# Layer 0's experts in a four-layer network: every expert's second product, or only the two that each image chose, fetched by register

## The reference

```
logits = jnp.mean(x, axis=1) @ Wr + br
routing_weights = jax.nn.softmax(logits, axis=-1)
scale = jnp.where(expected_loads > capacity, capacity / expected_loads, 1.0)
routing_weights = jax.nn.softmax(routing_weights * scale, axis=-1)
rw_tok = jnp.broadcast_to(routing_weights[:, None, :], (B, S, E)).reshape(N, E)
top_w, top_i = jax.lax.top_k(rw_tok, K)
top_w = jax.nn.softmax(top_w, axis=-1)
xf = x.reshape(N, D)
h = jax.nn.gelu(jnp.einsum('nd,edf->enf', xf, W1) + b1[:, None, :], approximate=False)
y = jnp.einsum('enf,efd->end', h, W2) + b2[:, None, :]
w_dense = jnp.zeros((N, E), x.dtype).at[jnp.arange(N)[:, None], top_i].add(top_w)
out = jnp.einsum('ne,end->nd', w_dense, y).reshape(B, S, D)
out = _layer_norm(out + x, gamma, beta)
```

## Time and profile before

| what | value |
|---|---|
| median of three runs | 211.53 us (211.3 to 212.07) |
| the profiled execution | 211.5 us, its span 209.7 us |
| TensorE busy | 195.9 us, 93% of the span |
| VectorE, ScalarE, GpSimd busy | 124.5, 129.3, 42.5 us |
| granted TensorE clock | 1.00 on average |
| logits of layer 0 to the first matmul of its norm 2 | 20.38 to 40.84 us |

### The profile page before, as it was taken

How to read it: one execution, slowest core, us unless ns; L and a number is a source line. 1 busy time by engine, 2 the same in 40 slices (tenths; PEclk the granted TensorE clock), 3 DMA queues, 4 the chain that set the end, 5 groups by cost and what they waited for, 6 DMA issues and landing times.

```text
span 209.7 us, 3083 instructions
## 1 busy us (share of the span) xinstructions
PE 195.9 (93%) x1112; PEld 91.5 (44%) x1120; DVE 124.5 (59%) x364; ACT 129.3 (62%) x216; POOL 42.5 (20%) x60
## 2 busy tenths in 40 slices
PE   7998999999999998999999999999998997799993
PEld 2654222348876764322222363532234594333221
DVE  0466879957641824945342547595455688586435
ACT  2535688646355683776575830688685675598682
POOL 7761000000000000103963000100920011010740
PEclk9999999999999999999999999999999999999999
DMA  6999300000000000000000000000000000000001
GB/s 228 355 407 404 123 0 2 0 0 3 2 3 0 3 0 0 0 5 0 0 0 0 0 3 0 0 0 0 0 6 0 2 0 3 0 0 0 3 0 50
DMA packets 3119, 8.40 MB, mean 40 GB/s; under 512 B 550, under 2 KB 1072, under 8 KB 2976
## 3 DMA queue, kind: packets, MB, share of 16 engines
q1 hardware_dynamic: 2736, 7.60, 9.7%
q0 software_dynamic: 224, 0.46, 0.6%
q10 hardware_dynamic: 144, 0.13, 0.2%
HBM read 7.94 MB, written 0.26 MB: 39 GB/s over the span
## 4 chain that ended last, share of the span: by engine, by line
PE 78%; DVE 10%; ACT 8%; issue 3%; DVEq 0%; ACTq 0%
PE bank L362 17%; PE banks L379 9%; PE banks L291 8%; PE banks L380 7%; PE banks L555 6%; PE bank L302 5%; PE bank L296 4%; ACT hidden L727 3%; PE bank L343 3%; PE banks L516 2%; PE banks L497 2%; PE bank L612 2%; PE bank L480 2%; PE bank L325 2%; ACT rstd L689 1%
## 5 line engine op out<-in xcount | busy, mean ns | idle before, releaser
L727 ACT ACTIVATE hidden<-banks,pack_l 128x1024 f32<-128x1024 f32 (+1 forms) x43 | 44.9, 1052 | 18.3 <-PE banks L380 17.8
L362 PE MATMUL bank<-hidden,w 128*64 128x512 f32 (+1 forms) x160 | 41.4, 596 | 1.3 <-ACT hidden L727 1.3
L291 PE MATMUL banks<-idle_work 128*128 128x512 bf16 x116 | 31.1, 401 | 2.0 <-DVE idle_work L1000 1.2
L379 PE MATMUL banks<-split_x,w_hi 128*128 128x512 f16 x80 | 30.7, 384 | 0.0
L380 PE MATMUL banks<-split_x,w_lo 128*128 128x512 f16 x80 | 30.3, 379 | 0.0
L1442 POOL CAST split_x<-normed 64x256 f16<-64x256 f32 x8 | 4.0, 494 | 99.7 <-DVE normed L896 95.2
L685 ACT ACTIVATE squares<-bank 128x256 f32<-128x256 f32 x18 | 6.9, 383 | 22.5 <-PE bank L296 22.4
L379 PEld LDWEIGHTS banks<-split_x,w_hi 128*128 128x128 f16 x80 | 7.7, 97 | 28.4 <-issue 11.5
L291 PEld LDWEIGHTS banks<-idle_work 128*128 128x128 bf16 x123 | 12.4, 105 | 16.2 <-issue 5.0
L1451 POOL TENSOR_TENSOR total<-total,term 128x512 f32<-128x512 f32 x12 | 17.6, 1463 | 2.6 <-DVE term L982 2.0
L362 PEld LDWEIGHTS bank<-hidden,w 128*64 128x64 f32 x160 | 7.9, 134 | 18.3 <-issue 13.6
(11 more groups left out here) (314 smaller groups left out, 322.3 us busy)
## 6 DMA issues: line engine op xcount, KB each, us to landing
w_stage<-in_w SPq DMA_DIRECT2D x3, 512.0 KB, 13.2
w_stage<-in_w SPq DMA_DIRECT2D x1, 1024.0 KB, 9.6
conv<-in_conv SPq DMA_DIRECT2D x1, 800.0 KB, 7.7
w<-in_w SPq DMA_DIRECT2D x3, 256.0 KB, 13.4
w<-in_w SPq DMA_DIRECT2D x1, 512.0 KB, 10.4
toeplitz<-in_toeplitz SPq DMA_DIRECT2D x1, 512.0 KB, 11.2
gauss<-in_gauss SPq DMA_DIRECT2D x1, 512.0 KB, 12.4
pack_l<-in_pack_l SPq DMA_DIRECT2D x1, 373.5 KB, 14.9
```

The source lines that it names most:

```text
L291: mm(out, idle_work[:, 0:128], idle_work[:, 0:cols], start=True, stop=True)
L362: last = mm(out[64 * h:64 * h + 64, cut], w2[l][:, (f * NE + e) * CH:(f * NE + e + 1) * CH], hidden[v % 3][:, h * 512 + cut.start:h * 512 ...
L379: mm(out, w1_hi[l][:, at:at + 128], split_x[h][:, :], start=True, stop=False)
L727: last = act(hidden[u % 3][:, cut], both[u % 2][:, cut], ACT.Gelu, bias=P(f"l{l}", "e_b1")[:, e * fc + f:e * fc + f + 1])
```

## The change

TensorE's stream for layer 0's experts is a new function, `image_experts`. The first products of all 8 experts are still made; units 0 and 1 use the fp32 weights and `normed[1]` directly (`STRAIGHT = 2`), so that they don't wait for the half-precision parts, and unit 0 stands ahead of the logits matmul. All eight hidden activations are kept, in `l0_hidden`. VectorE finds the two best experts of each image with its sorting and index instructions. GpSimd reads the eight chosen numbers (4 images by 2) into registers and copies for each the 128x64 block of `w2` into a zeroed 128x128 stationary (`w2_pick`); the zero columns let both halves accumulate into one 128-row result. TensorE reads the same eight numbers into registers of its own, and makes eight 256-column fp32 matmuls in place of sixteen 512-column ones; their moving operand's address comes from the register. VectorE weighs four results in place of sixteen. ScalarE has no biases to add and no `split`, which goes wholly to GpSimd; the second bias is brought into norm 2 by two matmuls of its own (L376). One softmax is left out of the routing and replaced by the order of the scaled values and a sigmoid of the gap.

```diff
-        hidden = [sb(f"hidden{i}", [128, 2 * COLS]) for i in range(3)]
+        l0_hidden = sb("l0_hidden", [128, EXPERTS * 2 * COLS])
+        hidden = [l0_hidden[:, i * 2 * COLS:(i + 1) * 2 * COLS] for i in range(3)]
...
+            def image_experts():
+
+                def up(u):
+                    pe.wait_ge(S["w1_loaded0"], 16)
+                    if u == 0:
+                        pe.wait_ge(S["ln_out"], 4)
+                    if u >= 2:
+                        pe.wait_ge(S["moe_gelu"], u - 1)
+                    if u == STRAIGHT:
+                        pe.wait_ge(S["w1_split0"], 2)
+                        pe.wait_ge(S["split_lo"], 4)
+                        for h in range(HALVES):
+                            pe.wait_ge(S[f"split_hi{h}"], 2)
+                    for h in range(HALVES):
+                        r, out = slice(64 * h, 64 * h + 64), both[u % 2][:, h * 512:(h + 1) * 512]
+                        cut = slice(u * 128, u * 128 + 128)
+                        if u < STRAIGHT:
+                            last = mm(out, stage[0][r, cut], normed[1][r, :], start=True, stop=True)
+                        else:
+                            mm(out, w1_hi[0][:, cut], split_x[h][:, :], start=True, stop=False)
+                            last = mm(out, w1_lo[0][:, cut], split_x[h][:, :], start=False, stop=True)
+                    last.then_inc(S["moe_hidden"], 1)
+
+                up(0)
+                pe.wait_ge(S["ones_set"], 1)
+                pe.wait_ge(S["routed"], 2)
+                mm(bank[7][:, 0:INNER * 16], ones[:, :], routed[:, :], start=True, stop=True)\
+                    .then_inc(S["route_logits0"], 1)
+                for u in range(1, NE):
+                    up(u)
+                    busy(1, bank[4][:, :])
+                pe.wait_ge(S["l0_index"], 2)
+                at = {(j, h, n): pe.value_load(own_at[64 * h:64 * h + 1, j * 8 + n:j * 8 + n + 1], min_val=0,
+                                               max_val=NE - 1)
+                      for j in range(INNER) for h in range(HALVES) for n in range(TOP_K)}
+                busy(5, bank[4][:, :])
+                pe.wait_ge(S["moe_gelu"], NE)
+                pe.wait_ge(S["w2_picked"], BATCH * TOP_K)
+                for j in range(INNER):
+                    for n in range(TOP_K):
+                        for h in range(HALVES):
+                            i = (j * HALVES + h) * TOP_K + n
+                            last = mm(picked_y[j][:, n * PIX:(n + 1) * PIX], tile(w2_pick, i),
+                                      l0_hidden[:, bass.ds(at[j, h, n] * (2 * COLS) + (h * COLS + j * PIX), PIX)],
+                                      start=h == 0, stop=h == 1)
+                    last.then_inc(S["l0_down"], 1)
+
+            def norm_of_images():
+
+                pe.wait_ge(S["l0_bias"], 1)
+                for j in range(INNER):
+                    mm(bank[4 + j][:, 0:PIX], P("first", "center"), gap["bias"][:, j:j + 1].broadcast_to([128, PIX]),
+                       start=True, stop=False)
+                for j in range(INNER):
+                    pe.wait_ge(S["l0_term"], 2 * j + 2)
+                    mm(bank[4 + j][:, 0:PIX], P("first", "center"), chunk(total, j), start=False, stop=True)\
+                        .then_inc(S["ln_centered"], 1)
+                averages(2)
...
-            split(1, 0)
...
+            nc.scalar.preload_act_table_set("gelu_and_others")
...
+            image_routing(0)
+            for u in range(NE):
+                sc.wait_ge(S["moe_hidden"], u + 1)
+                act(l0_hidden[:, u * 2 * COLS:(u + 1) * 2 * COLS], both[u % 2][:, :], ACT.Gelu,
+                    bias=P("l0", "e_b1")[:, u:u + 1]).then_inc(S["moe_gelu"], 1)
+                if u in (2, 5):
+                    image_routing((2, 5).index(u) + 1)
...
+            for j in range(INNER):
+                st.mark(V.max(own["sorted"][:, j * 8:j * 8 + 8], own["scaled"][:, j * 8:j * 8 + 8]))
+            ve.wait_ge(st.sem, st.n)
+            TT(g8(own["shifted"][:, :]), g8(own["sorted"][:, :]), g8(own["sorted"][:, :])[:, :, 0:1]
+               .broadcast_to([128, INNER, 8]), ALU.subtract).then_inc(S["l0_exp_in"], 1)
+            for j in range(INNER):
+                V.max_index(own_at[:, j * 8:j * 8 + 8], own["sorted"][:, j * 8:j * 8 + 8], own["scaled"][:, j * 8:j * 8 + 8])\
+                    .then_inc(S["l0_index"], 1)
...
+            for j in range(INNER):
+                ve.wait_ge(S["l0_down"], j + 1)
+                for n in range(TOP_K):
+                    if n:
+                        ve.wait_ge(S["l0_term"], 2 * j + 1)
+                    STT(chunk(total, j), picked_y[j][:, n * PIX:(n + 1) * PIX], pair["weight"][:, j * TOP_K + n:j * TOP_K + n + 1],
+                        chunk(total if n else normed[1], j), ALU.mult, ALU.add).then_inc(S["l0_term"], 1)
...
+            G.memset(w2_pick[:, :], 0.0).then_inc(S["picks_zero"], 1)
...
-            split(1, 0)
+            for j in range(INNER):
+                po.wait_ge(S["ln_out"], 2 * 1 + j + 1)
+                for h in range(HALVES):
+                    r = slice(64 * h, 64 * h + 64)
+                    G.tensor_copy(chunk(split_x[h], j)[r, :], chunk(normed[1], j)[r, :]).then_inc(S[f"split_hi{h}"], 1)
+            po.wait_ge(S["w2_loaded0"], 16)
+            po.wait_ge(S["l0_index"], 2)
+            for j in range(INNER):
+                for h in range(HALVES):
+                    for n in range(TOP_K):
+                        i = (j * HALVES + h) * TOP_K + n
+                        at = po.value_load(own_at[64 * h:64 * h + 1, j * 8 + n:j * 8 + n + 1], min_val=0, max_val=NE - 1)
+                        G.tensor_copy(w2_pick[:, i * 128 + 64 * h:i * 128 + 64 * h + 64], w2[0][:, bass.ds(at * CH, CH)])\
+                            .then_inc(S["w2_picked"], 1)
```

More of the change, by code:

```diff
@@ L167, in metaformer @@
         routed = sb("routed", [128, INNER * 16])
[L168 to L173, removed]
+        l0 = {n: sb(f"l0_{n}", [128, 32]) for n in "logit shifted prob".split()}
+        l0_small = {n: sb(f"l0s_{n}", [128, 8]) for n in "peak sum inv load scale".split()}
+        own = {n: sb(f"own_{n}", [128, INNER * 8]) for n in "scaled sorted shifted exp less inverse index".split()}
+        own_at = sb("own_at", [128, INNER * 8], mybir.dt.uint32)
+        pair = {n: sb(f"pair_{n}", [128, INNER * TOP_K]) for n in "bias weight part".split()}
+        chosen = {n: sb(f"chosen_{n}", [128, INNER * TOP_K * 8]) for n in "mask bias".split()}
+        gap = {n: sb(f"gap_{n}", [128, INNER]) for n in "sum inv less diff tanh bias".split()}
+        relu_sim, sq_sim = (l0_hidden[:, i * 2 * COLS:(i + 2) * 2 * COLS] for i in (3, 5))
         x1_beta = sb("x1_beta", [PART, COLS])
@@ L318, in experts @@
             def experts(l, k):
                 fc, base = fc_of[l], unit_base[l]
[L321 to L328, removed]
+                pe.wait_ge(S["ln_out"], 2 * k + 2)
@@ L329, in experts @@
+                pe.wait_ge(S[f"l{l}_loaded"], 16)
+                for i in range(TILES):
+                    last = mm(bank[7][:, i * 16:(i + 1) * 16], tile(normed[k], i), P(f"l{l}", "router"),
+                              start=True, stop=True)
+                last.then_inc(S["route_logits"], 1)
+                busy(1, bank[0][:, :])
                 pe.wait_ge(S[f"w1_split{l}"], 2)
@@ L427, in _ @@
             norm(1, x[1], x_ready(1))
[L428 to L432, removed]
+            image_experts()
+            norm_of_images()
             for j in range(INNER):
@@ new lines, in _ @@
+            st.mark(rsum(gap["sum"][:, :], g8(ex)))
+            st.link(TS(gap["less"][:, :], ex[:, 1::8], -1.0, 1.0, ALU.mult, ALU.add))
+            st.link(V.reciprocal(gap["inv"][:, :], gap["sum"][:, :]))
+            TT(gap["diff"][:, :], gap["less"][:, :], gap["inv"][:, :], ALU.mult).then_inc(S["l0_exp_in"], 1)
+            ve.wait_ge(S["l0_index"], 2)
+            st.link(V.tensor_copy(own["index"][:, :], own_at[:, :]))
+            masks = lambda n: chosen[n][:, :].rearrange("p (b k e) -> p b k e", b=INNER, k=TOP_K)
@@ new lines, in _ @@
+            st.link(TT(masks("mask"), P("l0", "order").unsqueeze(1).unsqueeze(1).broadcast_to([128, INNER, TOP_K, 8]),
+                       g8(own["index"][:, :])[:, :, 0:TOP_K].unsqueeze(3).broadcast_to([128, INNER, TOP_K, 8]), ALU.is_equal))
+            st.link(TT(g8(chosen["bias"][:, :]), g8(chosen["mask"][:, :]), repeat(P("l0", "e_b2"), INNER * TOP_K), ALU.mult))
+            st.link(rsum(pair["bias"][:, :], g8(chosen["bias"][:, :])))
+            ve.wait_ge(S["l0_exp"], 3)
+            for n in range(TOP_K):
+                st.mark(TS(pair["weight"][:, n::TOP_K], gap["tanh"][:, :], 0.5 - n, 0.5, ALU.mult, ALU.add))
```

111 lines of the change are left out of this document (38 added, 73 removed).

## The result

The changed kernel takes 216.04 us (median of four, 215.4 to 216.2) against 211.42 for the kernel before in its four runs: ratio 1.021, 95% interval 1.019 to 1.024. It is slower by 4.6 us, where 2.2 less was forecast. The profiled execution took 215.4 us, its span 213.6 us, 3.9 more than before.

What follows compares the result with a forecast made beforehand. TensorE was taken as the bound, about 1.95 us per expert. Second products from 34.3 plus 5.4 us put the end of centring at 39.7 against 41.86, so 211.5 - 2.2 = 209.3 us, range 207.4 to 212.9.

Steps and rivals of the forecast that it cites:

- What bounds before, and what the new structure saves: Layer 0's experts: TensorE bounds at about 1.95 us per expert; centring ends 2.2 us earlier and everything behind moves along.
- Up to the indices: Layer 0's routing ahead of the reads: VectorE's first routing instruction at 21.35, `l0_index` complete at 27.3 us.
- The new stall of ScalarE ahead of its second exponential: Behind GELU 2, ScalarE waits for the exponential's input until 26.9: 1.3 us, with TensorE's further units queued behind.
- I assume that its sequencer goes on while the array works through unit 7: TensorE's reads start at 30.4, without waiting for unit 7's matmuls; otherwise 0.8 us more.
- T = 0.35: Time in us of one register read with its two bounds checks; eight in series on TensorE take 2.8 us.
- 5.0 - 8T: Gain in us for T, one checked read's time: used up at T = 0.62, loss over 0.5% from 0.75.
- the dear reads' slower side: Checked reads of 0.75 us or more between unit 7 and the second products: loss over 0.5%, chance 0.07 of 0.18.
- signs of being wrong: New profile: GpSimd's last copy after 34, second products at 32.4, reads of 0.6 or more, clock under 1.00, late `conv_lo`.
- The clock, given 0.08 as a rival by itself: TensorE idle 2.1 us behind unit 7 drops to 1.2 GHz; second products cost 3.45 us more: 212.8 us, chance 0.08.
- From D to C: From the second products' start to the end of layer 0's centring: 5.4 us, VectorE's later jobs just hidden before norm 2.
- GpSimd late: GpSimd's register-addressed copies cost 0.8 in place of 0.25 us, delaying second products to 36.5: 211.5 us, no change, chance 0.07.

Runs made afterwards that it cites:

- e1: The changed kernel with fixed operand addresses in place of TensorE's register reads, so wrong experts are mixed; GpSimd's reads stay: 209.85 us, ratio 0.992 to the kernel before.
- e7: The changed kernel, reads unchecked, TensorE's two behind each of units 4 to 7, logits matmul before unit 0, second exponential behind GELU 3: 206.98 us, ratio 0.977 to before.
- e2: The changed kernel with both bounds checks left out of every register read on TensorE and GpSimd: 211.36 us, ratio 0.999 to the kernel before.
- e9: The changed kernel with 3 and 4 more idle matmuls ahead of TensorE's two waits for VectorE's weights in layer 3: 215.17 us.
- e8: The changed kernel with TensorE reading only the four first choices, checked, each used twice, so second choices are wrong: 210.92 us, ratio 0.996 to the kernel before.

## Why the prediction was wrong, step by step

**What bounds before, and what the new structure saves: right.** TensorE set the pace and the stage's end moved the rest. With no reads on TensorE the time fell below that of before (e1), and with cheap, covered reads to 206.98 against 211.73 (e7).

**Up to the indices: right within 0.3 us.** Logits on VectorE at 21.65 (forecast 21.35), indices complete at 27.41 (27.3). The new stall of ScalarE ahead of its second exponential was 0.76 us, not 1.3, because GELU 2 itself came 0.7 late. GELU 5 ended at 30.69 (30.2), the last at 33.02 (32.4): 0.5 and 0.6 late.

**"I assume that its sequencer goes on while the array works through unit 7": right.** The first read starts with unit 7's first matmul, at 30.86; the forecast had 30.4, and GELU 5's half microsecond is all of the difference.

**"T = 0.35": the step that failed.** A read with its checks measured 0.75 us on TensorE in the changed kernel, and 0.81 on GpSimd. The read alone is 0.465, more than the whole of T, and the two checks add 0.285 (e2), which I had counted as nearly free beside a DMA issue's 0.43. Eight times 0.40 are 3.2 us. By the forecast's own formula, 5.0 - 8T, this alone turns the gain of 2.2 into a loss of 1.0: the dear reads' slower side, which had 0.07. Three of the signs of being wrong that the prediction names came: reads over 0.6, a granted clock under 1.00 and a last copy of GpSimd after 34 (34.09).

The Trainium skill's two figures, about 200 ns in "Runtime: NRT & Kernel Launch" (Instruction fetch mechanics) and 600 ns in "DMA: Bandwidth & Descriptors" (Latency and other measured facts), enclose the 0.465 us of the unchecked read measured here (e2). Neither fits it, neither speaks of checks, and the checked read's 0.75 is over both.

**The clock, given 0.08 as a rival by itself: it came, behind the dear reads.** The prediction reckoned it with a standstill of 2.1 us; the reads made it 4.76. It cost 1.0 on the five idle matmuls and 0.5 on the second products in the profiled run. The fall in layer 3, which no step had, cost 1.0 more (0.9 in e9).

The forecast end of centring was 39.7. Adding 0.46 (GELU chain, and with it the start of the reads), 3.18 (8T, 5.98 for 2.8), 1.03 and 0.49 (clock) gives 44.86; the trace has 44.82. Against 41.86 that is 3.0, with layer 3's fall 3.9 to 4.0; the spans differ by 3.9. The medians differ by 4.6, since the profiled run was the fastest of the four.

**From D to C: right.** 5.4 forecast; 5.87 measured, 0.5 of it clock; in e7 5.5. `conv_lo` ended when norm 2 wanted VectorE: its first multiplication starts 1.3 us after centring, 1.36 before. **GpSimd late: did not happen,** though its reads cost 0.81 each; its copies took 0.24 for 0.25 and ran beside the reads, which the forecast had put in series.

What the prediction lacked was a view of the two together. It gave the reads' price and the clock separate chances, but a dearer read lengthens the very standstill that brings the clock down.

## What to carry to other kernels

A value read into a register cost TensorE's stream nearly half a microsecond here, and three quarters with its two bounds checks. The timeline puts this time down to "issue"; a query of the line shows the rows. Count reads one by one and place them where the engine waits anyway, two unchecked ones where the cover is 1 us. When a stream stands still on TensorE, price the clock with it: the matmuls behind the standstill, filler included, may run at half speed. When a change loses, take its suspected cost away by itself before giving up the structure; here the same idea with other placement and order ended 2.3% below the kernel before.

## What the runs showed that I had not expected

- Two bounds checks add 0.285 us to a read of 0.465 on TensorE, and 0.29 to one of 0.52 on GpSimd.
- Reads of the same kind differ: loads of 0.30 to 0.31 us where the read before took the column beside, 0.46 to 0.49 where it took another partition or chunk. Leaving out four reads saved 0.63 each because they were the short ones (e8); a price worked out from a difference holds only for what was left out.
- A longer standstill is not the surer fall: 2.48 us kept the full clock behind it (e2), 2.24 us had it at 0.50 from about 35.5 (e8), 1.32 kept it (e1). From such rows no safe length can be given.
- The kernel before has a mean clock of 0.992 in 9 of 46 runs, and takes about 1.5 us longer in them; in its profiled run no wait of TensorE behind the start is over 1.0 us. Covering layer 3's waits with idle matmuls removed the late fall in e9's trace; how often it would do so was not tried.
